# Probabilities of two wide attention layers turned by VectorE and DMA instead of TensorE

## The reference

```python
def attention(x, ctx, Wq, Wk, Wv, Wo, bo):
    q = (x @ Wq).reshape(b, n, H, DH)
    k = (ctx @ Wk).reshape(b, m, H, DH)
    v = (ctx @ Wv).reshape(b, m, H, DH)
    sim = jnp.einsum('bihd,bjhd->bhij', q, k) * SCALE
    attn = jax.nn.softmax(sim, axis=-1)
    out = jnp.einsum('bhij,bjhd->bihd', attn, v).reshape(b, n, H * DH)
    return out @ Wo + bo
h = layer_norm(x, ln1_g, ln1_b)
x = x + attention(h, h, Wq1, Wk1, Wv1, Wo1, bo1)
h = layer_norm(x, ln2_g, ln2_b)
x = x + attention(h, context, Wq2, Wk2, Wv2, Wo2, bo2)
```

## Time and profile before

| | |
|---|---|
| Median of 3 runs | 1851.69 us (1851.04 to 1851.97) |
| The profiled execution | 1851.2 us, of which the span of the profile is 1849.5 us |
| TensorE busy | 1788.7 us (97%) |
| VectorE busy | 1361.6 us (74%) |
| ScalarE busy | 1239.4 us (67%) |
| GpSimd busy | 678.3 us (37%) |
| The two wide layers | from 8.03 us (first turned norm) to 849.4 us |

### The profile page before, as it was taken

The page is one execution under the profiler, slowest core; times in us unless marked ns, Lnnn a source line. Parts: engine busy times, 40 slices in busy tenths (PEclk is TensorE's granted clock), DMA queues, the critical chain, the costliest instruction groups (busy, mean ns, idle before and its releaser), DMA issues. The chain is left out here.

```text
span 1849.5 us, 51513 instructions
## 1 busy us (share of the span) xinstructions
PE 1788.7 (97%) x18056; PEld 1511.2 (82%) x18056; DVE 1361.6 (74%) x2600; ACT 1239.4 (67%) x3858; POOL 678.3 (37%) x946
## 2 busy tenths in 40 slices
PE   8999999999999999998989999998999999999997
PEld 6888888888888888887967777787888888888885
DVE  5676776767676776766768888658888888888886
ACT  4666666666666666664348888446777777778786
POOL 3343333444444434433322222444343434343431
PEclk9999999999999999999999999999999999999999
DMA  8100000000000000000000000000000000000000
GB/s 222 34 0 0 0 0 0 0 1 2 2 0 0 0 0 0 1 1 1 0 1 1 0 0 0 1 0 2 5 5 3 4 3 4 3 4 3 5 4 9
DMA packets 18745, 14.92 MB, mean 8 GB/s; under 512 B 4514, under 2 KB 16356, under 8 KB 18660
## 3 DMA queue, kind: packets, MB, share of 16 engines
q1 hardware_dynamic: 18660, 13.78, 2.8%
HBM read 11.68 MB, written 2.10 MB: 7 GB/s over the span
## 5 line engine op out<-in xcount | busy, mean ns | idle before, releaser
L815 POOL TENSOR_TENSOR L_probs<-L_probs,L_inv_sum 128x1024 f32<-128x1024 f32 x128 | 242.7, 1896 | 330.1 <-DVE L_inv_sum L716 330.1
L610 ACT ACTIVATE L_qT<-L_ring 128x512 f32<-128x512 f32 x128 | 76.5, 597 | 251.8 <-PE L_ring L498 251.8
L721 DVE COPY L_v<-L_ring 128x512 f32<-128x512 f32 x128 | 88.6, 692 | 194.2 <-PE L_ring L526 194.2
L619 ACT ACTIVATE L_probs<-L_scores,L_neg_max 128x128 f32<-128x128 f32 x512 | 181.4, 381 | 6.4 <-DVE L_neg_max L696 6.4
L690 DVE TENSOR_REDUCE L_row_max<-L_scores 128x8 f32<-128x1024 f32 x128 | 153.5, 1199 | 26.6 <-PE L_scores L480 26.6
L610 ACT ACTIVATE L_probsT<-L_ring 128x512 f32<-128x512 f32 x256 | 139.0, 597 | 20.9 <-PE L_ring L490 20.9
L1536 ACT ACTIVATE L2L_w_probs<-L2L_scores,L2L_w_neg_max 128x128 f32<-128x128 f32 x256 | 92.0, 395 | 77.1 <-DVE L2L_w_neg_max L1694 77.1
L537 PEld LDWEIGHTS L_ring<-L_probsT,L_v 128*64 128x64 f32 x2048 | 110.5, 137 | 32.0 <-issue 23.6
L490 PE MATMUL L_ring<-ident,L_probs 128*128 128x128 f32 x1024 | 133.3, 273 | 3.2 <-POOL L_probs L815 3.1
L1904 POOL TENSOR_TENSOR L2L_w_probs<-L2L_w_probs,L2L_w_inv_sum 128x1024 f32<-128x1024 f32 x64 | 121.3, 1896 | 33.1 <-DVE L2L_w_inv_sum L1730 33.1
L480 PE MATMUL L_scores<-L_kT,L_qT 64*128 64x128 f32 x2048 | 131.5, 279 | 1.0 <-ACT L_probs L619 1.0
(11 more groups left out here) (224 smaller groups left out, 4929.8 us busy)
## 6 DMA issues: line engine op xcount, KB each, us to landing
out_x<-x SPq DMA_DIRECT2D x32, 64.0 KB, 1.5
L0a_wq<-in_L_xattn_Wq SPq DMA_DIRECT2D x2, 256.0 KB, 2.7
L0a_wk<-in_L_xattn_Wk SPq DMA_DIRECT2D x2, 256.0 KB, 3.3
L0a_wv<-in_L_xattn_Wv SPq DMA_DIRECT2D x1, 512.0 KB, 6.1
L0a_wo<-in_L_xattn_Wo SPq DMA_DIRECT2D x1, 512.0 KB, 6.7
L0b_wq<-in_L_xattn_Wq SPq DMA_DIRECT2D x1, 512.0 KB, 4.8
L0b_wo<-in_L_xattn_Wo SPq DMA_DIRECT2D x1, 512.0 KB, 7.0
wp<-in_L_xattn_Wp SPq DMA_DIRECT2D x1, 512.0 KB, 6.5
```

What stands on the lines that cost most here:

```text
L610: nc.scalar.activation(to, src, ACT.Copy).then_inc(emptied["act"], 1)
L619: done = nc.scalar.activation(slot_probs(at, 0)[:, n, :], scores[:, 0, r, i, :], ACT.Exp, scale=layer_of(at).scale, bias=neg_max[:, n:n + ...
L721: nc.vector.tensor_copy(v[:, at.n % 2, BANK * n:BANK * (n + 1)], bank(f"v{n}", at)).then_inc(emptied["dve"], 1)
L815: nc.gpsimd.tensor_tensor(to, to, inv_sum[:, :, s, :].unsqueeze(3) .to_broadcast([TOKENS, 2, GROUP, TOKENS]), ALU.mult).then_inc(divided, 1)
```

## The change

The 16 transposes per item on TensorE and the four copies on ScalarE go. Instead VectorE's `turn_squares` turns each 32x32 square of the probabilities within itself, a slot at a time, into `squares`, and SyncE's new `spread` issues 16 DMAs per item, one for each square of the 4x4 grid and all 16 heads, which move 32 partitions of `squares` to the 32 partitions of `probsT` where they belong (64 KB each, 2 KB a partition). Both tiles have two halves for alternate items. `landed` is the wait for an item's 16 DMAs. The copies of values and of weighted values go from VectorE to ScalarE. The scores of an item and all behind them up to the division are made two steps ahead of its weighting instead of one, the projections four instead of three. The loads of later weights are issued in pieces between the spreads.

```diff
-        def later_loads(sp):
+        def later_loads(sp, t):
-            for w in ("q", "k"):
...
+            if t == BATCHES - 7:
+                load_norm(sp, "L0b", "ln2", "L0_xattn_ln2_g", "L0_xattn_ln2_b")
+                load_wide(sp, "L0b", "L0b", "2", CTX)
+            if t == BATCHES - 3:
...
+            if t == 2 * BATCHES:
+                load_norm(sp, "L2", "L2_ln", "L2_xattn_gamma", "L2_xattn_beta")
+                load_wide(sp, "L2", "L2", "", CTX)
...
-    order = [("qa", 3, "act"), ("ka", 3, "act"), ("Wo", -1, "dve"), ("T0", 0, "act"), ("T1", 0, "act"),
-             ("qb", 3, "act"), ("kb", 3, "act"), ("T2", 0, "act"), ("T3", 0, "act"),
-             ("v0", 1, "dve"), ("v1", 1, "dve"), ("hT", 5, "dve"), ("PV0", 0, "dve"), ("PV1", 0, "dve")]
+    order = [("v0", 1, "act"), ("v1", 1, "act"), ("hT", 5, "dve"), ("Wo", -1, "dve"), ("qa", 4, "act"),
+             ("ka", 4, "act"), ("qb", 4, "act"), ("kb", 4, "act"), ("PV0", 0, "act"), ("PV1", 0, "act")]
+    SQUARE = 32
+    SQUARES = TOKENS // SQUARE
+    LANDED = 16 * SQUARES * SQUARES
...
-        probsT = sb("probsT", [TOKENS, HEADS, TOKENS])
+        squares = sb("squares", [TOKENS, 2, SQUARES, HEADS, SQUARE])
+        probsT = sb("probsT", [TOKENS, 2, SQUARES, HEADS, SQUARE])
...
-        block.sync(sync_program)
+        def landed(engine, at):
+
+            engine.wait_ge(probsT_landed[at.n % 2], at.times(LANDED // 2, LANDED - LANDED // 2 * (at.n % 2)))
+
+        @block.sync
+        def _(sp):
+            def spread(at):
+                p = at.n % 2
+                sp.wait_ge(squares_turned, at.times(2, 2))
+                if at.n >= 2:
+                    await_filled(sp, "PV1", at.plus(-2))
+                for i in range(SQUARES):
+                    for j in range(SQUARES):
+                        sp.dma_start(probsT[SQUARE * j:SQUARE * (j + 1), p, i, :, :],
+                                     squares[SQUARE * i:SQUARE * (i + 1), p, j, :, :]).then_inc(probsT_landed[p], 16)
+
+            for t in range(first, last + 1):
+                sync_program(sp, t)
+                if here(At(t), 1):
+                    spread(At(t + 1))
...
-            def transpose_probs(at, n):
...
-                await_emptied(pe, f"T{2 * s + 1}", at)
+                landed(pe, at)
...
-                                                probsT[:, SLOT_HEADS * s + GROUP * r + i, :],
+                                                probsT[:, at.n % 2, :, SLOT_HEADS * s + GROUP * r + i, :],
...
+                    if at.n >= 2:
+                        act.wait_ge(squares_turned, at.times(2, -3))
...
-            def turned_probs(at, n):
...
+            def values(at, n):
+                await_filled(act, f"v{n}", at)
+                copied(v[:, at.n % 2, BANK * n:BANK * (n + 1)], bank(f"v{n}", at))
+
+            def weighted(at, s):
+                await_filled(act, f"PV{s}", at)
+                copied(oT[:, GROUP * s:GROUP * (s + 1), :].rearrange("p c t -> p (c t)"), bank(f"PV{s}", at))
...
+                if here(t, 2):
+                    exponentiate_0(t.plus(2), 0)
+                if here(t, 1):
+                    values(t.plus(1), 0)
+                    values(t.plus(1), 1)
+                if here(t, 2):
+                    exponentiate_0(t.plus(2), 1)
+                if here(t, 4):
+                    projections(t.plus(4), 0)
+                if here(t, 2):
+                    exponentiate_1(t.plus(2))
+                if here(t, 4):
+                    projections(t.plus(4), 1)
...
+            def turn_squares(at, s):
+                dve.wait_ge(divided, at.times(2, s + 1))
+                if at.n >= 2:
+                    landed(dve, at.plus(-2))
+                nc.vector.transpose(squares[:, at.n % 2, :, SLOT_HEADS * s:SLOT_HEADS * (s + 1), :]
+                                    .rearrange("p j h a -> p h j a"),
+                                    slot_probs(at, s).rearrange("p h (j b) -> p h j b", b=SQUARE)
+                                    ).then_inc(squares_turned, 1)
...
+                if here(t, 2):
+                    divide(t.plus(2), 0)
+                if here(t, 7):
+                    inverse_deviation(t.plus(7))
+                if here(t, 2):
+                    divide(t.plus(2), 1)
```

More of the change, by code:

```diff
@@ L345, in wide_attention @@
     weights_step = items - 1
-    other_orders = {t: order[:2] + [(f"ctx{n}", 0, "act") for n in groups] + order[2:] for t, groups in turns.items()}
+    other_orders = {t: order[:8] + [(f"ctx{n}", 0, "act") for n in groups] + order[8:] for t, groups in turns.items()}
     other_orders[weights_step] = [("weights", 0, "dve")] + order
@@ L598, in step @@
                     transpose_h(t.plus(5))
+                if here(t, -1):
+                    project_out(t.plus(-1))
+                if here(t, 4):
+                    queries_keys(t.plus(4), 0)
+                    queries_keys(t.plus(4), 1)
+                if t.i is None:
+                    for n in turns.get(t.n, ()):
+                        turn_context(t, n)
                 if here(t, 0):
@@ L643, in step @@
             def step(t):
-                if here(t, 3):
-                    projections(t.plus(3), 0)
+                if here(t, 2):
[9 more added lines that the diff above has]
+                    exponentiate_1(t.plus(2))
+                if here(t, 4):
+                    projections(t.plus(4), 1)
                 if t.i is None:
@@ L648, in step @@
                         turned_context(t, n)
[L649 to L650 removed]
                 if here(t, 0):
[L652 to L661 removed]
+                    weighted(t, 0)
+                    weighted(t, 1)
             steps(act, step)
@@ L818, in step @@
             def step(t):
-                if here(t, 0):
-                    divide(t, 1)
-                if here(t, 7):
-                    inverse_deviation(t.plus(7))
-                early_context = here(t, 5) and layer_of(t.plus(5)).from_context
-                if early_context and not here(t, 1):
+                if here(t, 5) and layer_of(t.plus(5)).from_context:
                     stage_context(t.plus(5))
```

168 lines of the change are left out of this document (58 added, 110 removed).

## The result

| | |
|---|---|
| Before | 1851.37 us median (1850.48 to 1851.97, 4 runs) |
| After | 1773.07 us median (1771.12 to 1775.10, 4 runs) |
| Ratio | 0.9578, 95% interval 0.9561 to 0.9594 |
| The profiled execution after | 1772.23 us, span 1770.1 us, mean granted clock 0.989 |

The kernel is 78 us faster; 101 were forecast. The time is inside the range of 1736 to 1798 us but above the band of 1738 to 1762 that was the forecast proper.

A forecast was written before the change was run, and what follows sets the result against it. TensorE was taken to bound the kernel, never waiting in the wide layers. From 1851.2 us, -112.0 for the transposes and +10 at the ends give 1749.2; the runs' median, 0.5 above, makes 1750 us, range 1736 to 1798.

The forecast's parts named there:

- two passes: Rival (14%): VectorE takes two passes over a block transpose, 2.45 us each; steps 11.6 to 11.8 us, time 1778 to 1797.
- smaller stalls: Rival (7%): late landings, strided operand or a ring bank stall TensorE 0.2 to 1.2 us a step: 1762 to 1830.
- The 16 transposes, -112.0: TensorE's step loses 1.75 us of transposes a batch, 64 times: -112.0 us, step 12.89 to 11.14 us.
- ScalarE's and VectorE's copies, zero: ScalarE swaps four copies for four of the same size, zero; VectorE loses those four, 2.77 us.
- The block transpose, 1.22 us: VectorE turns 128x1024 fp32 twice a batch, 1.22 us each as a plain stream; bounds 0.69 and 2.45.
- VectorE's chain with 0.3 us to spare: VectorE's in-order step ends at 12.0 us, next maxima can start at 12.3, so TensorE stays the bound.
- An issue on SyncE, 0.48 us: SyncE's 16 issues a batch take 7.7 us of a step of 11.14; slack before weighting 3.9 us, so zero.
- Landing, 1.5 us: A batch's squares, issued by 15.0, land 1.5 us later, a 64 KB store's time, ahead of TensorE's weighting.
- The moved loads, "zero, up to +4": Seven second-layer loads ahead of one spread on SyncE's queue delay its landing a microsecond at most: zero, up to +4.
- The operand in four runs, zero: Weighting's moving operand becomes four runs of 32 columns: taken as zero, from zero to twice its 1.90 us.
- The ends, +10: Start +5, last steps' idle +4 and one more for steps without projections: +10 together, from 0 to 20.
- The rival on SyncE: Rival (12%): SyncE's queue is the bound; at 0.85 us an issue steps take 13.6 us, 1895 to 1920 us.

The follow-up runs named there:

- run from HBM: The changed kernel's 16 DMAs a batch read rows of a weight in HBM instead of the squares, result meaningless: 1757.39 us.
- One load a step: Against the changed kernel, the 34 later loads go out one a step from step 1, ahead of the step's spreads: 1764.13 us.
- four issues: Against the changed kernel, 4 DMAs of 128 partitions x 2 KB a batch instead of 16, same bytes, wrong rows weighted: 1745.12 us.
- 12 and 4: Against the changed kernel, GpSimd issues 4 of a batch's 16 DMAs and SyncE the other 12: 1753.13 us.
- 8 and 8: Against the changed kernel, GpSimd issues 8 of a batch's 16 DMAs and SyncE 8: 1767.75 us.
- the two runs that tried it: Small matmuls fill TensorE's waits before the last weightings: in the changed kernel 1769.53 us; with GpSimd issuing 4 of the 16 DMAs 1753.03 us.
- six on GpSimd: Against the changed kernel, GpSimd issues 6 of a batch's 16 DMAs and SyncE 10: 1753.35 us.

## Why the prediction was right, and where it was not

The sign, the steady step and most of the gain are right, for the reasons given. That the time is inside the range is in part luck: the forecast's own band ended at 1762, and the range reached further for rivals, of which that of two passes did not happen. What happened, landings that come late, is named among the smaller stalls (7%), but there as a loss in every step; it was one at the loads and in the tail. Of the signs of being right two failed, issues under 0.5 us apart and no idle time before weighting.

- **The 16 transposes, -112.0.** Right: the steady step is 11.15 us, forecast 11.14.
- **ScalarE's and VectorE's copies, zero.** Right: no row of TensorE's steady step waits.
- **The block transpose, 1.22 us.** Right: 1225 ns. The rival of two passes (2.45) is out. The Trainium skill, "VectorE: DVE Perf Modes", section on the three transpose paths, gives 311 ns for a bf16 block of 128x128, by which eight would be near 2.5, an estimate; the fp32 rows here show half of that.
- **VectorE's chain with 0.3 us to spare.** Right in sign, too small in size: a transpose more a step, 1.22 us, left the steady step as it was and cost 8 us over the run.
- **An issue on SyncE, 0.48 us. This is the step that failed.** I took it from loads out of HBM and from a store to it; with both ends in SBUF it is 0.632 start to start, so 10.1 us and not 7.7 of each step. It stays under the 0.70 at which I had SyncE bound the step, and nothing shows in the steady state. But of the slack of 3.9 us before weighting 2.4 (16 x 0.15) and 0.5 (landing) were not there, which leaves about 1 us (1.5 in the trace) for what stands ahead in the queue, two or three issues of loads and not eight. The run from HBM puts the forecast's price into the same 16 issues (0.42 busy, 7.3 us a batch): 1757.39 us. So this step is worth 15.7 of the 23 us between forecast and result.
- **Landing, 1.5 us.** Mis-sized: 2.0.
- **The moved loads, "zero, up to +4".** It was +9.2 (7.9 of waits, 1.3 of clock). The seven loads that I priced cost 3.04, inside my bound; the 16 loads that stand ahead of the other three waits I had left out. One load a step removed all four. It hangs on the issue's price: with sources in HBM the same loads in the same places cost nothing.
- **The operand in four runs, zero.** Right: 1.90 us.
- **The ends, +10.** The start, +5, was +4.5: the trace agrees, no run tried it alone. The tail, +5, was about +17 with another 2 us behind it. I had its chain but not that SyncE's 10 us repeat in each of the short last steps, nor that the turning waits there for the output projection; with four issues the tail lost 17 us of this. The clock, which my sum left out, made six groups longer by 6.9 us together (0.63, 0.96, 1.40, 1.31, 1.71, 0.93), but gave back only 3.5.
- **The rival on SyncE** (slower from 0.79 us) came half true: the right resource, at a price that hurts only where the step is shorter or the queue carries more.

With the four wide issues, which take 2.4 us a batch and not the forecast's 7.7, the time is 1745, 5 us under the forecast of 1750: its wide layers end at 739.7, 109.7 us earlier than before, so that start and tail together cost 2.3 us rather than 10. The Trainium skill, "DMA: Bandwidth & Descriptors", gives in its section on the anatomy of a DMA some 2.0 us fixed for one issued by GpSimd, mostly completion; the landing of 2.0 us for 64 KB, issued by SyncE, is near it, and the issues 0.63 us apart show again that it overlaps. The advice of its section on bandwidth to make DMAs large came true in another way, by the count of issues on one engine.

## What to carry to other kernels

Price a DMA issue by a row with the same two ends (here HBM to SBUF 0.42 us, SBUF to HBM 0.33, SBUF to SBUF 0.59), multiply by the count, and compare with the shortest step that it must fit in, not the steady one, and with the time from the last landing to its reader; a queue that is 90% full in the steady state has room for a load now and then, not for eight in a row. Two engines issuing, 12 and 4, was worth 20 us here and 8 and 8 only 5: the second engine's own work is then late. Matmuls at a lower clock inside a wait for another engine cost little in the two runs that tried it; they count behind the last wait, and where the next work of the awaited engine hangs on them.

## What the runs showed of the hardware

- A DMA issue on SyncE costs by where its ends are: 0.591 us between SBUF and SBUF, 0.421 from HBM. Between SBUF and SBUF it doesn't go with partitions (32 or 128), row length (512 B to 2 KB) or bytes (32 to 256 KB). GpSimd's issue of the same transfer costs 0.498 us of GpSimd, and the landings of both together keep their median of 2.0 us.
- A transfer of 256 KB between partitions landed in 2.5 us, of 64 KB in 2.0, of 32 KB in 1.8.
- VectorE's 32x32 block transpose of 128x1024 fp32 runs at the speed of a plain stream, 1225 ns.
- After the tail's waits of 2 to 5 us TensorE's next group ran partly at the lower clock (2.6 to 3.7 us for 1.97), at a granted clock of 0.80 over the tail; with 8 to 22 small matmuls in each wait it stayed at 1.00. It isn't so behind every wait: after 3.04 us at 341.52, and after 3.15 and 2.61 us with four issues on GpSimd, the group took 1.97.
- Both issuers can pause at once: with six on GpSimd, its third issue of the last item came 2.17 us late while one of SyncE's took 1.66 us instead of 0.59, from 737.9 us. A 16 KB packet of the instruction queue stands there too (737.72, 1.4 us). So it does beside every spread's issue over 1.0 us on SyncE between 60 and 800 us, 17 in the changed kernel and 2 (four issues) to 18 in the others; that the packet is the cause is not shown.
